# Dealing PE's work over the turns of a tile: projection, values and gates of a talking-heads attention kernel

## What is computed

```python
q, k, v = heads(x @ Wq), heads(x @ Wk), heads(x @ Wv)        # 16 heads of 64, x is layer-normed
k, v = concat([mem_k, k]), concat([mem_v, v])                # 4 memory rows ahead
q, k = l2norm(q), l2norm(k)
dots = einsum('bhid,bhjd->bhij', q, k) * 10.0
dots = einsum('hg,bgij->bhij', W_pre_th, dots)               # mix over heads
dots = causal(dots); keep the 64 largest of each row
attn = softmax(dots)
attn = einsum('hg,bgij->bhij', W_post_th, attn)              # mix over heads again
out = einsum('bhij,bhjd->bhid', attn, v) * head_scale
out = out * sigmoid(x @ Wg + bg)                             # the gates
x = x + out @ Wo                                             # the projection
```

## Time and profile before

| | |
|---|---|
| median of three runs | 2406.95 us |
| the profiled execution | 2402.8 us |
| its span, first to last instruction | 2401.0 us |
| PE, matmuls | 2104.1 us busy (88%), 16059 instructions |
| PE, weight loads | 1363.1 us (57%) |
| DVE | 1801.4 us (75%) |
| ACT | 1622.8 us (68%) |
| POOL | 812.5 us (34%) |
| mean granted TensorE clock | 0.955 |
| before the attention phase's first mix | 238.6 us |
| last projection ends, about | 2183 us |

### The profile page before, as it was taken

One profiled execution on the slowest core, in us unless ns is written; L12 is line 12 of the kernel. 1 busy time (PEld: TensorE's weight loads), 2 busy tenths in 40 slices (PEclk: granted clock), 3 DMA queues, 4 the chain that ended last, 5 costly groups with the idle time before them and its releaser, 6 DMA issues. The chain is left out here.

```text
span 2401.0 us, 55203 instructions
## 1 busy us (share of the span) xinstructions
PE 2104.1 (88%) x16059; PEld 1363.1 (57%) x16060; DVE 1801.4 (75%) x7282; ACT 1622.8 (68%) x4700; POOL 812.5 (34%) x2274
## 2 busy tenths in 40 slices
PE   7995789898999998899989988998898889884997
PEld 3433456665566556665666666666666666563433
DVE  6564489868986898689868986898689868983446
ACT  4442578757876787678767885888588758871543
POOL 3001444344434433443344334433443344311000
PEclk9996899999999999999999999999999999997998
DMA  5002012101210121012101210121012101212001
GB/s 171 0 9 75 22 38 60 42 25 42 59 42 25 42 60 42 25 42 60 42 25 42 60 42 25 42 59 42 25 42 60 42 23 40 57 37 85 0 1 70
DMA packets 113218, 104.71 MB, mean 44 GB/s; under 512 B 34448, under 2 KB 110864, under 8 KB 112912
## 3 DMA queue, kind: packets, MB, share of 16 engines
q1 hardware_dynamic: 108000, 96.65, 15.8%
q10 hardware_dynamic: 4912, 4.46, 0.6%
HBM read 19.14 MB, written 12.71 MB: 13 GB/s over the span
## 5 line engine op out<-in xcount | busy, mean ns | idle before, releaser
L1491 DVE TENSOR_SCALAR_CACHE_REDUCE S<-S,minus_thr 128x68 f32<-128x68 f32 (+56 forms) x456 | 218.0, 514 | 225.6 <-POOL minus_thr L1388 224.8
L1048 PE MATMUL bankC<-R,E 128*128 128x128 f32 x2560 | 349.9, 286 | 34.6 <-POOL R L1395 34.6
L1048 PEld LDWEIGHTS bankC<-R,E 128*128 128x128 f32 x2560 | 337.3, 201 | 70.7 <-POOL R L1395 36.7
L1032 PE MATMUL bankB<-raw,mixpre 128*128 128x76 f32 (+37 forms) x1024 | 357.8, 437 | 19.3 <-DMA raw<-SC 19.2
L1244 ACT ACTIVATE S<-bankB,aim_first 128x68 f32<-128x68 f32 (+56 forms) x456 | 231.2, 510 | 201.5 <-PE bankB L1032 199.7
L1379 POOL TENSOR_TENSOR S<-S,diagmask 128x8 f32<-128x8 f32 x512 | 108.6, 216 | 688.2 <-ACT S L1244 654.7
L1022 PE MATMUL bankD<-KT,QT 64*64 64x258 f32 (+7 forms) x2304 | 195.6, 409 | 94.2 <-ACT SC L1233 86.0
L1395 POOL TENSOR_SCALAR R<-mixpost,rinv 128x128 f32<-128x128 f32 x512 | 184.8, 374 | 180.1 <-DVE rinv L1555 179.7
L1551 DVE SCALAR_TENSOR_TENSOR E<-S,limit,E 128x68 f32<-128x68 f32 (+56 forms) x456 | 221.2, 521 | 30.4 <-DVE E L1551 0.3
L1270 ACT ACTIVATE E<-S,nmax 128x12 f32<-128x12 f32 (+56 forms) x512 | 233.2, 505 | 14.5 <-POOL nmax L1409 14.5
L1074 PEld LDWEIGHTS bankM<-PT,V 128*64 128x64 f32 x5120 | 183.9, 141 | 102.4 <-issue 85.9
(11 more groups left out here) (176 smaller groups left out, 3968.8 us busy)
## 6 DMA issues: line engine op xcount, KB each, us to landing
X_first<-in_L_attn_x_dram ACTq DMA_DIRECT2D x8, 512.0 KB, 9.6
x<-X_first SPq DMA_DIRECT2D x8, 512.0 KB, 2.9
xt<-x SPq DMA_DIRECT2D x32, 128.0 KB, 2.4
x<-xt SPq DMA_DIRECT2D x32, 128.0 KB, 2.5
X_last<-x SPq DMA_DIRECT2D x8, 512.0 KB, 6.6
out_dram<-X_last SPq DMA_DIRECT2D x8, 512.0 KB, 2.8
raw<-SC SPq DMA_DIRECT2D x8, 258.0 KB, 3.0
raw<-SC SPq DMA_DIRECT2D x8, 254.0 KB, 3.5
```

What stands on the lines that cost most here:

```text
L1032: last = nc.tensor.matmul(bankB[n % 2][:, 0:wide(n)], W.mixpre[:, :], raw[n % RAWS][:, 0:wide(n)], start=True, stop=True)
L1048: last = nc.tensor.matmul(bankC[n % 2][:, jb * P:(jb + 1) * P], E[n % EBUFS][:, jb * P:(jb + 1) * P], R[n % RBUFS][:, :], start=True, stop ...
L1491: nc.vector.tensor_scalar(row, row, minus_thr[:, col(n)], None, ALU.add, ALU.max, accum_out=rmax[:, col(n)]).then_inc(max_done, 1)
```

## The change

`PROJECT_AT` goes from 8 to 6, `V0_AT` from 4 to 2, and `GATES_AT` from 6 in every tile to 12 in a batch's first tile and 10 in the others. `gates` takes a half: half 0 is issued in the turn that `GATES_AT` names and half 1 in the turn after, on PE and on ACT. The list of uses follows; the values of a batch's first tile now stand between pieces 0 and 1 of turn 2's scores. On DVE `ln_stats` moves from turn 2 to turn 0. No instruction is added or left out.

```diff
--- before.py
+++ after.py
@@ -26,9 +26,9 @@
 RBUFS = 4
 XBUFS = 6
 GBUFS = 3
-PROJECT_AT = 8
-GATES_AT = (6, 6, 6, 6)
-V0_AT = 4
+PROJECT_AT = 6
+GATES_AT = (12, 10, 10, 10)
+V0_AT = 2
 V1_AT = 2
 LAG = 6
 RAWS = 6
@@ -863,11 +863,13 @@
                 if g == 0 and ahead:
                     uses += [("xT", t + 1, 0)] + two("q", t + 1)
                 if g == 2:
-                    uses += score_steps(2 * t + 1, 0) + score_steps(2 * t + 1, 1)
+                    uses += score_steps(2 * t + 1, 0)
                 if g == 4:
                     uses += score_steps(2 * t + 1, 2)
                 if early_values(t, g):
                     uses += two("v", t)
+                if g == 2:
+                    uses += score_steps(2 * t + 1, 1)
                 if g == 4 and ahead:
                     uses += two("k", t + 1)
                 if g == 6:
@@ -880,8 +882,8 @@
                     uses += score_steps(2 * t + 2, 1) + score_steps(2 * t + 2, 2)
                 if g == 14 and ahead:
                     uses += score_steps(2 * t + 2, 3)
-                if g == gates_turn(t):
-                    uses += two("g", t)
+                if g - gates_turn(t) in (0, 2):
+                    uses.append(("g", t, (g - gates_turn(t)) // 2))
                 if values_at(t, g):
                     uses += two(*values_at(t, g))
         place = {u: i for i, u in enumerate(uses)}
@@ -984,17 +986,17 @@
                         return last
                     pe_use(pe, (what, j, half), emit)
 
-            def gates(j):
+            def gates(j, half):
                 x = xnT[j % 2]
-                for half in range(2):
-                    def emit():
-                        for q in range(4):
-                            for k in range(2):
-                                lo = (4 * half + q) * P
-                                last = nc.tensor.matmul(bankD[:, half, q * P:(q + 1) * P], Wg[:, k, lo:lo + P],
-                                                        x[:, k, MEM:MEM + P], start=k == 0, stop=k == 1)
-                        return last
-                    pe_use(pe, ("g", j, half), emit)
+
+                def emit():
+                    for q in range(4):
+                        for k in range(2):
+                            lo = (4 * half + q) * P
+                            last = nc.tensor.matmul(bankD[:, half, q * P:(q + 1) * P], Wg[:, k, lo:lo + P],
+                                                    x[:, k, MEM:MEM + P], start=k == 0, stop=k == 1)
+                    return last
+                pe_use(pe, ("g", j, half), emit)
 
             def turn_qk(j, i, what):
                 pe.wait_ge(qk_ready, 2 * j + i + 1)
@@ -1141,8 +1143,8 @@
                         score(2 * t + 2, 0)
                     if g == 12 and ahead:
                         score(2 * t + 2, 2)
-                    if g == gates_turn(t):
-                        gates(t)
+                    if g - gates_turn(t) in (0, 2):
+                        gates(t, (g - gates_turn(t)) // 2)
                     if values_at(t, g):
                         what, j = values_at(t, g)
                         if what == "v":
@@ -1198,17 +1200,17 @@
                     act.dma_start(V[0:MEM, slot(j), :].rearrange("m (h d) -> m h d", d=DH),
                                   a["mem_v"].rearrange("h m d -> m h d")).then_inc(mem_in, 16)
 
-            def gates(j):
-                if j >= GBUFS:
+            def gates(j, half):
+                if j >= GBUFS and half == 0:
                     act.wait_ge(projected, j - GBUFS + 1)
-                for half in range(2):
-                    def emit():
-                        for q in range(4):
-                            pair = 4 * half + q
-                            last = nc.scalar.activation(gate[j % GBUFS][:, pair, :], bankD[:, half, q * P:(q + 1) * P],
-                                                        ACT.Tanh, bias=W.bgh[:, pair:pair + 1], scale=0.5)
-                        return last
-                    act_use(act, ("g", j, half), emit)
+
+                def emit():
+                    for q in range(4):
+                        pair = 4 * half + q
+                        last = nc.scalar.activation(gate[j % GBUFS][:, pair, :], bankD[:, half, q * P:(q + 1) * P],
+                                                    ACT.Tanh, bias=W.bgh[:, pair:pair + 1], scale=0.5)
+                    return last
+                act_use(act, ("g", j, half), emit)
 
             def qT(j):
                 for half in range(2):
@@ -1581,7 +1583,7 @@
                 if 2 <= n0 and n0 + 2 < NG:
                     row_max(n0 + 2)
                     row_max(n0 + 3)
-                if g == 2 and t + 2 < NT:
+                if g == 0 and t + 2 < NT:
                     ln_stats(t + 2)
                 select_pair(n0)
                 if g == 6 and t + 2 < NT:
```

## The result

The changed kernel takes 2581.6 us (median; the kernel before, beside it, 2406.8). The ratio is 1.072, with a 95% interval of 1.069 to 1.075: slower, as forecast, but by 175 us where 74 were forecast, and outside the range. One of its four runs, at 2624.3 us and a granted clock of 0.900, is left out of the ratio as disturbed. The profiled execution took 2575.8 us, its span is 2574.0, so 173.0 us more than before's 2401.0.

What follows compares the result with a forecast made beforehand. PE, busy 215.6 of a batch's 239.3 us, sets the pace. Terms 17.9 - 2.7 - 1.8 - 3.0 - 0.8 = +9.6 us a batch, +74 in all, gave about 2480 us from 2407, 3.1% slower; range 2430 to 2525.

Steps and rivals of the forecast that it cites:

- The waits of the halves: Gates' halves behind end-of-turn scores (turns 10, 12) wait for ACT's copy: 54 waits, 17.9 us a batch, 137 in all.
- The clock: the step that failed: PE's slow matmuls after stalls, some 1.4 us each: two such places go, two come, so no net change.
- two longest idle stretches: Argument from the earlier trace: PE's two longest idle stretches are followed by slow matmuls, the 2.27 us one isn't.
- Rival D: Slow clock after every PE stall: seven less two at 1.4 us, 16.6 us a batch, 2537 us; chance 0.07.
- The wait for R at the start of T0: PE's 2.98 us wait for R, DVE's lateness, goes since a later PE no longer meets it: -3.0 us a batch.
- The transposes' wait for POOL: Earlier row statistics bring T1's k transposes 0.8 us sooner: -0.8 us a batch; other tiles 0.
- gates ... behind them wait for POOL in any case, so I count nothing: ACT no longer reads gates before the q transposes; k transposes wait for POOL anyway: 0, possibly 0.5 us a tile.
- Project: Projection from turn 8 to 6, 3.62 us a tile, takes the place gates leave, on bankT: cost nothing.
- Turn 14 and the raw rows: Turn 14's mid-turn score waits go (2.7 us a batch); T0's second half covers T1's raw rows' wait (1.8 us).
- Values and statistics: T0's values to turn 2: 0, bounds 2.27 us either way; DVE's row statistics to turn 0: 0.8 us gained in T1.

Runs made afterwards that it cites:

- the waits alone: Kernel before, nothing moved; PE only waits at the end of turns 10 and 12 (12 in T0) for ACT's score copy: 2604.8 and 4087.9 us, no ratio.
- The fillers: Changed kernel plus matmuls whose result nobody reads, in four fifths of each stall of turns 10 and 12: 2513.7 us, ratio 1.049.
- Gates alone: Kernel before with only the gates' product moved, in two halves at turns 12 and 14 (T0), 10 and 12 (T1 to T3): 2682.4 us, ratio 1.116.
- the rest alone: Kernel before with project in turn 6, T0's values in turn 2, row statistics in turn 0, gates whole in turn 6: 2379.7 us, ratio 0.991.

## Why the prediction was right or wrong

The direction, the mechanism and its largest term were right; the size was wrong, and the result lies outside the range.

- **The waits of the halves.** Forecast 54 waits and 137 us; measured 54 and 135.6. The gates read from the earlier trace rows, with a product in a like place in the earlier trace rows to back them, held. That the wait is PE's in the order of work, and not a matter of what is moved, is shown by the waits alone (+202 us). The turns moved as forecast, or a little more: in T2 turn 10 is 4.8 us longer, turn 12 6.0, and turn 8 is 2.9 shorter.
- **The clock: the step that failed.** I let two slow stretches go and two come, "no net change", and said that PE's busy sum would stay within 1%. It rose by 3.6%, 74.8 us. I had seen that a 2.27 us stall wasn't followed by slow matmuls, and took the length of a gap as what decides. My own rows spoke against that: the raw rows' gap of 1.78 us was shorter, and slow matmuls followed it, so it is wrong that the "two longest idle stretches" are the slow ones. The changed kernel shows it plainly. The very stall of the earlier trace rows is there again, as long as before:

```profile
1355.75 5.37 PE L984 MATMUL bankD<-Wv,xnT 128*128 128x512 f32 x8 [2.27 <-ACT SC L1235]
```

  The eight matmuls took 3.67 us in all eight batches before; now they take 5.37 in seven of the eight. Of the 54 halves of the gates that follow a wait, 37 took 2.66 to 3.78 us and 17 took 2.05. Among the 14 waits of 1.2 to 2 us, 10 are followed by a slow half; among the 14 over 2.9 us, 13 are. T2's half above took 2.05 us after an idle 2.75. So the length of one gap doesn't tell which half is slow; more idle places in a batch did bring more time at the lower level, and what decides each single case stays open. An estimate from the mean granted clock, 0.955 and 0.926: the time at the lower of the two levels is 2 x 0.045 x 2401 = 216 us before and 2 x 0.074 x 2574 = 381 us after; 165 us more, at half speed worth up to 82. The fillers show it: all 53 halves that still wait, for 0.4 us on average, take 2.05 us, and 56 to 68 us come back. Rival D took a rule of the Trainium skill ("TensorE: Matmul & The Clock Gate", section "HAM oscillation — how this bites in real kernels"), which is for idle gaps that are long enough, and stretched it to every stall. It was right in that more stalls mean more slow matmuls, and its price of 7 us a batch was close to the 9.4 measured, but 17 of the 54 halves contradict it as a rule. Its chance of 0.07 was too low.
- **The wait for R at the start of T0.** Forecast gone (3.0 us a batch, 21 us). It is 29.6 us of 34.6 still. "A later PE no longer meets it" was wrong because it isn't R that is awaited there any more:

```profile
1286.63 0.30 PE L1034 MATMUL bankB<-raw,mixpre 128*128 128x20 f32 x2
...
1289.59 2.02 PE L1050 MATMUL bankC<-R,E 128*128 128x128 f32 x16 [2.67 <-ACT PT L1282]
...
1288.88 1.06 ACT L1282 COPY PT<-bankC 128x512 f32<-128x512 f32 x2
```

  PE's last turn of T3 is short, it runs ahead of ACT, and then stands for ACT's PT copies. DVE was late before, ACT is late now. This is read from the rows, not tried.
- **The transposes' wait for POOL.** Forecast -0.8 us a batch by the earlier statistics, and nothing for the rest. It rose by 24.3 us, with 15.7 of the tanh wait gone, so +8.6 instead of -6.4. T1's k transposes, for which 0.6 us were forecast, wait 1.46 us; T0's wait 2.09 (1.14 before) and T2's 1.47 (0.41). The sentence "gates ... behind them wait for POOL in any case, so I count nothing" was right on the tanh wait alone. Left out was that the gates in turn 6 are cover for that wait.
- **Project.** "Cost nothing" was the wrong price for its place in itself: it gives 27 us (ratio 0.988) where the gates stay, because it joins them as cover. In the full change it only takes over the cover that the gates gave up. Gates alone and the rest alone, +280 and -23 us, don't add up to the +175 of the whole. They share this cover, but that is only a part of it: from gates alone to the whole change the span falls by 119.4 us, of which 43.7 are the wait for POOL, 38.9 the raw rows' wait and 32.3 PE's busy time.
- **Turn 14 and the raw rows.** Forecast -21 and -14 us; measured -29.6 (all the scores' waits) and -14.3.
- **Values and statistics.** Nothing for the values, right. The statistics' gain in T1 was there when they moved alone, and its loss in T2 was missed; alone they cost 0.2%, most of it in PE's busy time.

The forecast's 74 us, with +75 for the clock, +16 for R's wait, +15 for the transposes and -8 for the scores, come to 172, and the spans differ by 173.0.

## What to carry to other kernels

Where two engines hand one buffer to and fro and each works in a fixed order, price a moved use by where its predecessor is read in the *reader's* order, not by how much work its new place has: behind an end-of-turn product it waits for the reader's whole turn. Before work is moved away, ask which wait it covers; making the turns more even gave nothing by itself here. And a stall of PE can cost twice, as it did here: 95.3 us more of waits came with 74.8 us more of busy time at a lower granted clock, and extra matmuls in the stalls won the second part back. Compare PE's busy sum in every run, since a step that seems to shorten a wait can pay by the clock instead.

## What the runs showed of the hardware

- The same stall of 2.27 us was followed by eight matmuls of 3.67 us in all in one kernel and of 5.37 in the other.
- More matmuls made the kernel faster: 121 us of them in PE's stalls raised the mean granted clock from 0.926 to 0.955 and took 68 us off the span.
- Shifting three small DVE instructions by 0.8 us gave nothing, as a DVE instruction that takes 0.23 us alone took 1.55 us beside POOL's 1.90 us product, where it had taken 0.78.
- With the waits alone the same matmuls were 112.5 us longer busy (2216.6 against 2104.1), at a mean granted clock of 0.909.
